# Products of no use on TensorE, at the borders of the stages and in attention's first pass

## What is computed

```
x = x + tanh(g) * cross_attention(layernorm(x), ctx)      # 16 heads of 16, rotary q and k, softmax
x = x + tanh(g) * experts(layernorm(x))                   # 8 routed (top 2) and 2 shared, inner width 128
x = x + tanh(g) * coattention(layernorm(x), ctx)          # similarity 512x512, pooled vector, W_qv
x = x + tanh(g) * ternary_ffn(layernorm(x))               # 256 -> 1024 -> 256, quantised rows and weights
```

## Time and profile before

| | |
|---|---|
| median of three runs | 749.66 us |
| profiled execution | 749.53 us, span 746.6 us |
| mean granted clock of TensorE | 0.938 of full |
| PE busy | 657.0 us, 88% of the span |
| DVE busy | 460.2 us, 62% |
| ACT busy | 341.0 us, 46% |
| POOL busy | 311.4 us, 42% |

### The profile page before, as it was taken

One profiled execution on the slowest core, in us unless ns is written; L12 is line 12 of the kernel. 1 busy time (PEld: TensorE's weight loads), 2 busy tenths in 40 slices (PEclk: granted clock), 3 DMA queues, 4 the chain that ended last, 5 costly groups with the idle time before them and its releaser, 6 DMA issues. The chain is left out here.

```text
span 746.6 us, 9638 instructions
## 1 busy us (share of the span) xinstructions
PE 657.0 (88%) x3251; PEld 410.7 (55%) x3270; DVE 460.2 (62%) x779; ACT 341.0 (46%) x596; POOL 311.4 (42%) x482
## 2 busy tenths in 40 slices
PE   5975899999999878788999999996899999956985
PEld 3543344344344247456777777773667675833553
DVE  3966888888888227478343433435465554449994
ACT  3445388888888853355232323422311212013664
POOL 8655658676543406500010100101131726256896
PEclk9997599999999979899999999997989998987999
DMA  8795766736400049001100000001000000000101
GB/s 264 170 247 220 153 74 84 94 55 80 51 1 1 1 164 344 14 1 54 74 1 0 2 0 0 1 0 56 1 0 1 1 1 0 1 0 0 35 29 50
DMA packets 22951, 43.39 MB, mean 58 GB/s; under 512 B 3868, under 2 KB 10656, under 8 KB 22144
## 3 DMA queue, kind: packets, MB, share of 16 engines
q1 hardware_dynamic: 15992, 32.59, 13.8%
q0 software_dynamic: 6048, 10.03, 10.1%
q10 hardware_dynamic: 872, 0.27, 0.2%
HBM read 32.27 MB, written 10.49 MB: 57 GB/s over the span
## 5 line engine op out<-in xcount | busy, mean ns | idle before, releaser
L673 DVE TENSOR_REDUCE mx<-ps_f 128x2 f32<-128x1024 f32 x128 | 151.5, 1220 | 26.6 <-PE ps_f L611 26.3
L776 ACT ACTIVATE prob<-ps_s 128x512 f32<-128x512 f32 x256 | 134.6, 608 | 34.2 <-PE ps_s L629 34.1
L629 PE MATMUL ps_s<-q_stacks,k_stacks 53*128 53x512 f32 x256 | 90.3, 484 | 5.7 <-ACT prob L776 3.3
L629 PEld LDWEIGHTS ps_s<-q_stacks,k_stacks 53*128 53x128 f32 x256 | 35.8, 188 | 86.9 <-ACT prob L776 70.6
L611 PE MATMUL ps_f<-k_stacks,q_stacks 53*128 53x512 f32 x256 | 64.8, 458 | 11.4 <-PEq L203 7.0
L638 PE MATMUL ps_o<-prob,vst 128*32 128x512 f32 x512 | 70.3, 624 | 0.0
L1254 DVE SCALAR_TENSOR_TENSOR h<-ps_u,most,qs 128x512 f32<-128x512 f32 x32 | 24.0, 750 | 62.7 <-ACT qs L1184 62.7
L168 POOL TENSOR_TENSOR norm_tmp_att<-st 128x4 f32<-128x4 f32 x4 | 1.0, 240 | 145.4 <-DVE st L1293 145.4
L1184 ACT ACTIVATE qs<-ps_g 128x512 f32<-128x512 f32 x40 | 23.9, 597 | 82.4 <-PE ps_u L1056 82.4
L700 POOL TENSOR_TENSOR q_stacks<-minus,q_stacks 128x1024 fp32r<-128x1024 f32 x16 | 38.0, 2373 | 37.6 <-ACT minus L767 37.6
L1714 ACT ACTIVATE qs<-ps_SC,nmax 128x512 f32<-128x512 f32 x16 | 11.0, 686 | 71.9 <-DVE nmax L1602 71.9
(11 more groups left out here) (289 smaller groups left out, 1466.3 us busy)
## 6 DMA issues: line engine op xcount, KB each, us to landing
k_stacks<-room_k POOLq DMA_DIRECT2D x18, 256.0 KB, 5.1
q_stacks<-room_q POOLq DMA_DIRECT2D x18, 256.0 KB, 5.3
up<-in_up SPq DMA_DIRECT2D x10, 256.0 KB, 6.7
x<-in_x SPq DMA_DIRECT2D x4, 512.0 KB, 9.7
ctx_raw<-in_ctxTC SPq DMA_DIRECT2D x4, 512.0 KB, 8.6
room_k<-k_high SPq DMA_DIRECT2D x4, 512.0 KB, 6.8
room_k<-k_low SPq DMA_DIRECT2D x4, 512.0 KB, 6.7
room_q<-q_high SPq DMA_DIRECT2D x4, 512.0 KB, 4.3
```

Of the source, the lines that this page charges most:

```text
L629: pe.matmul(ps_s[n % 3][:, :], ks[rows(h), 2 * s + pair, kt * P:(kt + 1) * P], qs[rows(h), 2 * s + pair, :], start=True, stop=True).then_i ...
L673: dve.tensor_reduce(mx[:, f % 2, qt, 2 * pair:2 * pair + 2], ps_f[n % 2][:, :, :], AX_X, ALU.max).then_inc(used, 1)
L776: act.activation(prob[:, kt % 2, j, :], ps_s[n % 3][:, :], ACT.Exp, scale=SCALE)\
```

## The change

Products whose results nobody reads are added to TensorE's program, nothing is removed.

- A helper `idle_products` multiplies a 128x128 float32 square by itself, `count` times, into a PSUM buffer that is not in use.
- In `phase_prepare` DVE clears one half of `xnT` as its first instruction and raises the new semaphore `idle_ready`. TensorE waits for it and makes 10 products of that half, 128x512, into `ps_q[0]`, ahead of its wait for the key weights.
- At the end of `phase_prepare` 24 products follow the last queries; they go into `ps_k[0]`, so they first wait for DVE's seventh raise of `parts`.
- In `phase_attend` 4 products follow each of the 14 units ahead of the steps, into `ps_o`, which the first values overwrite later.
- 6 products end `phase_attend`, 20 end `phase_project`, 14 end `phase_experts`, 8 end `phase_coattend`, and 22 begin `phase_bitffn`, ahead of its first transposes.

```diff
+def idle_products(pe, out, square, count):
+
+    for _ in range(count):
+        pe.matmul(out, square, square, start=True, stop=True)
...
# phase_prepare, tensor
+            pe.wait_ge(idle_ready, 1)
+            for _ in range(10):
+                pe.matmul(ps_q[0][:, :], xnT[:, 0, 0:P], xnT[:, 0, :], start=True, stop=True)
             pe.wait_ge(wk_in, 16)
             keys(0)
...
                 queries(b)
+            pe.wait_ge(parts, 2 * B - 1)
+            idle_products(pe, ps_k[0][:, 0:P], id32, 24)
# phase_prepare, vector
+            dve.memset(xnT[:, 0, :], 0.0).then_inc(idle_ready, 1)
             dve.wait_ge(x_in[0], 16)
# phase_attend, tensor
             for n in range(UNITS + 2):
                 first_scores(n)
+                idle_products(pe, ps_o[:, 0:P], id32, 4)
             maxima(0)
             for n in range(UNITS + 2, LEAD):
                 first_scores(n)
+                idle_products(pe, ps_o[:, 0:P], id32, 4)
...
             values(STEPS - 1, QT - 1)
+            idle_products(pe, ps_f[0][:, 0, 0:P], id32, 6)
# phase_project, tensor
             project(B - 1)
+            idle_products(pe, ps_t[0][:, 0, :, :].rearrange("p j c -> p (j c)"), id32, 20)
# phase_experts, tensor
             y_transposes(B - 1)
+            idle_products(pe, ps_g[0][:, 0:P], id32, 14)
# phase_coattend, tensor
                 features(B - 1, (B - 1) % 2, q)
+            idle_products(pe, ps_S[0][:, 0:P], id32, 8)
# phase_bitffn, tensor
+            idle_products(pe, ps_y[0][:, 0:P], per["c32"][:, C_ID:C_ID + P], 22)
             x_transposes(0, 0)
```

More of the change, by code:

```diff
@@ L225, in phase_prepare @@
         x_in, consts, weights = [sem("first_x_in"), sem("second_x_in"), sem("x_in")], sem("consts"), sem("weights")
-        trig_in, preset = sem("trig_in"), sem("preset")
+        trig_in, preset, idle_ready = sem("trig_in"), sem("preset"), sem("idle_ready")
         wk_in, ctx_in = sem("wk_in"), [sem("ctx_in0"), sem("ctx_in1")]
```

## The result

The changed kernel takes 751.25 us (median of 15 runs, 746.22 to 756.63), the kernel before in the same comparison 748.09 (15 runs, 742.75 to 750.97). The ratio is 1.0061, 95% interval 1.0034 to 1.0088: 4.6 us more by the ratio, 3.2 by the medians, where 3.25 less were forecast. The prediction had given slower a chance of 0.12. The profiled execution is at 751.4 us (span 749.6), mean granted clock 0.972 instead of 0.938: so the products do to the clock what they are meant to do, and the time goes up all the same.

The account below looks back on a forecast made before the run. TensorE's clock, at 1.2 instead of 2.4 GHz in attention's first 27 us and at stage borders, was taken as the bound. Terms 0.8 + 0.3 - 0.35 - 1.6 - 2.1 - 0.3 = -3.25 us gave 746.3 us, range 740.5 to 753.5.

Parts of the forecast that it names:

- the first pass: Attention's units ahead of the steps: 1.33 us each with four products, against DVE's 1.14; next maxima 0.3 us later.
- The price of a product: One f32 128x128 product on TensorE: 0.213 to 0.25 us at full clock, taken as 0.225.
- the step behind it: Attention's step after the first pass: at full clock, 5.4 us to the next maxima.
- Rival (b): Products outlast the gaps at start, first pass and borders, from about 0.24 us each: +4.3, 753.9 us; chance 0.15.
- Start, +0.8: Prepare's start: ten products delay the first keys, which then run faster; 0.8 us lost, bounds 0 and +2.1.
- Attention's end, -0.35: Attention-projection border: 0.55 us later from six products, 0.9 regained in projection's transposes; bounds +0.7 and -1.4.
- Projection's end, -1.6: Projection-experts border: 2.3 us gained in transposes and router, 0.7 lost to products outlasting POOL; bounds +1.2 and -2.3.
- Rival (c): Clock doesn't stay up behind the borders, where transposes with pauses follow: +2.15, 751.7 us; chance 0.10.
- the rule behind it: Trainium skill's rule that transposes don't count as clock activity like products; three borders starting with transposes would keep little.
- Experts' end, -2.1: Experts-coattention border: 2.6 us gained in transposes and half of the similarities, 0.5 lost; bounds +0.8 and -4.3.
- Last border, -0.3: Last stage's start: transposes 1.8 us late, hidden; 0.5 won in next tile's gate and up, 0.2 lost; bounds +0.9, -1.7.

Follow-up runs that it names:

- experiment 7: Kernel before plus only the 24 products at prepare's end and four per unit of attention's first pass: 751.52 us, ratio 1.0064.
- experiment 1: Changed kernel without the four products behind each of the 14 first-pass units: 746.85 us, ratio 0.9988 to the kernel before.
- experiment 5: Kernel with border products alone, plus three repeated 53-row score products per first-pass unit: 752.93 us over nine runs; ratio 0.9989, carried by three.
- experiment 13: Kernel before plus products at two borders only, 15 at projection's end and 11 at experts' end: 744.66 us, ratio 0.9948.
- experiment 14: Kernel with trimmed border products (6), plus 24 behind the first gate and up products of the last stage: 741.36 us, ratio 0.9913.
- experiment 8: Kernel before plus only the start's ten products, with their memset and wait: 749.61 us, ratio 1.0029.
- experiment 2: Changed kernel without the start's ten products, their memset and wait: 753.84 us, ratio 1.0074 to the kernel before.
- experiment 3: Changed kernel with two products per first-pass unit instead of four: 747.46 us; ratio 0.9961 without the upper group of runs.
- 10: The kernel of experiments 9 with the 24 products at prepare's end back: 749.37 us; ratio 0.9990 without the upper four of twelve runs.
- 6: Changed kernel without start, unit and prepare's-end products, other border products cut to 2, 15, 11 and 13, coattention's 8 kept: 743.76 us, ratio 0.9973.
- experiments 9: Kernel with trimmed border products (6), plus three 128-row products of a constant tile per first-pass unit: 750.76 us, ratio 1.0069.
- experiment 12: Changed kernel again, unchanged, for a second profile: 749.36 us.

## Why the prediction was wrong

**The step that failed: the first pass, "0.43 + 4 x 0.225 = 1.33 us a unit", +0.3.** The price of a product was right (0.23 us, 24 in a row), and so was the step behind it at full clock (5.5 us, forecast 5.4). But that price is one of a run of like products. Between scores of 53 rows, each group of four costs 0.17 us more, and 14 groups 2.4. So the steps begin 5.6 us late, not 3, and the maxima of step 1 are 3.0 us late instead of 0.3; 4.5 in the second profile, where the clock falls in step 0, and 6.0 in that of experiment 7, where it falls in the pass. Experiment 7 has the whole of the loss (4.5 us in the medians), experiment 1 gives it back (4.4). The 0.43 for the scores came out by luck: it fits two products one after the other (2 x 0.216), but the two run side by side (experiment 5), and among their like a pair takes 0.23 to 0.33 us. The rows that I took the price from the earlier trace rows have no change of shape in them, and I bounded the price by the product alone. Rival (b), products at 0.24 us or more, is what came in the first pass: as placed they cost 0.272 each. It also added losses at every border, and most of those did not come.

A second reason was in the rows before the prediction: DVE paced the pass. A faster clock had nothing to give there but the one step behind it, 2.6 us; anything that makes a unit longer than 1.14 us is paid fourteen times.

**Start, +0.8.** The mechanism came as told: twenty records from 1.45 to 11.96, the keys at full clock behind them, ended at 15.4 against 14.5. The first records of the changed kernel:

```profile
1.45 10.51 PE L330 MATMUL ps_qA<-xnT 128*128 128x512 f32 x20 [1.45 <-DVE xnT L378]
11.80 3.60 PE L299 MATMUL ps_k<-ctx_raw,wk 128*128 128x512 f32 x8
```

What is left of the 0.9 us at the end can't be read from prepare, whose length runs from 69.9 to 73.6 us over all profiles.

**Attention's end, -0.35.** Six products held the border up by about 0.9 us (the project's program began at 274.7), and the first groups of projection were at full clock. But the gain was counted against one execution, and the second profile of before has it without the products, while experiment 13, also without them, has the low clock again and 37.8 us.

**Projection's end, -1.6.** Right in mechanism and nearly in size: the group of transposes behind the router comes 2.0 us sooner after the border (4.2 for 6.3; forecast 2.3), and 0.9 us are lost to products that outlast POOL (forecast 0.7), which leaves -1.1. The whole experts' stage is 1.4 us shorter than in the first profile of before, 3.2 than in the second, with its own loss below in it. Rival (c) and the rule behind it did not come true here: sixteen transposes and the router behind the border ran at full clock (1.07, 1.14). By the Trainium skill, page "TensorE: Matmul & The Clock Gate", section "Part 4: PE-mode transpose", transposes do not count as activity in the way products do. This trace does not test whether they would raise the clock; the clock that the products had kept up stayed up for the 2.4 us of them.

**Experts' end, -2.1.** The transposes took 1.21 instead of 1.94, the similarities 8.98 instead of 10.31: the clock fell again at 516.8 us, just behind the wait for DVE that ended at 516.5. The beginning of coattention:

```profile
513.37 1.21 PE L1492 MATMUL ps_TC<-c,ks 128*128 128x128 f32 x8 [1.18 <-DVE ks L1604]
516.51 8.98 PE L1503 MATMUL ps_SC<-ks 128*128 128x512 f32 x16 [1.94 <-DVE ks L1614]
```

Coattention is 0.6 to 1.5 us shorter; but it is 148.1 us, shorter still, in experiment 7 without any product there, so this gain is not shown to be the products'. The fourteen products ended at 512.18, DVE at 511.51: 0.65 us of the experts' stage lost to them (forecast 0.5).

**Last border, -0.3.** No gain: the last stage is 86.4 and 84.4 us with them, 84.9 and 84.4 without. The first transposes are 1.65 us later in the stage, hidden, as told; then TensorE waits 4.29 us for POOL and the clock falls. The pause was named in the prediction; experiment 14 points to it, and not the border, as the place where products belong, by one profile each.

**The sum.** In the profiles (span 746.6 to 749.6) the stages add 2.4, 2.4, -1.3, -1.4, -0.6 and 1.5 us. Of these, prepare's and the last stage's lie within what two profiles of one kernel differ by. In the medians: the first pass +4.4 (experiment 1); the other products together, borders and start, 0.1% faster in the same experiment, which is no change clear of noise; the borders alone 0.4% faster, so the start may take some of it, which experiment 8 allows.

Open: the start's price; why the change of rows costs; why the clock fell at or soon behind attention's border after 24 products in some executions (experiments 2, 3, 5, 7, 10) and not in both profiles of the changed kernel; and how much of the gain of experiment 14 over 6 is its own, since their ratios come from different chips (0.9913 and 0.9973, the intervals overlap). The last stage gives it 1.3 us in one profile each.

## What to carry to other kernels

In these runs a product of no use was free only where TensorE waited, and its price is to be taken where it will stand: between work of another shape it is dearer than in a row of its own kind. Look first which engine paces the stretch; a low clock under a pass that VectorE paces costs nothing in the pass itself. And take two profiles before counting a gain by removing a low stretch of the clock: some of them belong to the execution and not to the kernel.

## What the runs showed of the hardware

- Four f32 products of 128x128 cost 0.92 us in a row and 1.09 between scores on 53 rows; three of 128x512 cost 0.25 us more than their own time in the same place, though of the same number form. At 1.2 GHz three products of 128x512 beside a pair of scores make a unit of 2.31 us on 128 rows and of 1.71 us on 53 (experiments 9 and 5). So the change of rows costs about 0.2 us there and back over the 0.43 of the pair.
- Two products on different rows run side by side: 75.02 and 75.03 us in experiment 5; among their like a pair of 512 columns takes 0.23 to 0.33 us at full clock.
- Work without a pause does not by itself keep or raise the clock: it was at 1.2 GHz for 32 us of unbroken work on 53 rows (experiment 5) and for 41 us in experiment 3, and in experiment 12 it fell at 95.9 us, with TensorE busy for 23.99 of the 24 us from 71 to 95.
- Executions of one kernel on one core differ by 1.6% (742.35 to 753.96 us in 35 runs of the kernel before). Where the clock falls differs between profiles of one kernel, and one stage was 6.4 us longer where it fell (experiment 2).
